# Results of six expert tiles kept in the join buffers, and another order of the row transfers on GpSimd, in a two-layer attention and mixture-of-experts kernel

## What is computed

```python
xn = _layernorm(x)
x = x + _L0_attn_ref(xn, ...) + _L0_ffn_ref(xn, ...)   # linear attention; top-2 of 8 experts, silu(hg) * hu, 176 wide, and a shared expert
xn = _layernorm(x)
x = x + _L1_attn_ref(xn, ...) + _L1_ffn_ref(xn, ...)   # masked linear attention per 256 tokens, rms norm, gate; top-2 of 8 experts, gelu, 512 wide
```

## Time and profile before

| | before |
|---|---|
| median of three runs | 919.67 us |
| profiled execution, its own time | 917.82 us |
| its span in the profile | 916.3 us |
| TensorE busy | 838.1 us, 91% |
| VectorE busy | 701.6 us, 77% |
| GpSimd busy | 625.9 us, 68% |
| ScalarE busy | 572.2 us, 62% |
| 224 sends, from L2014 | 220.8 us, 986 ns each |
| 136 returns, from L2116 | 151.8 us, 1117 ns each |
| 128 gathers, from L2025 | 132.7 us, 1036 ns each |

### The profile page before, as it was taken

One profiled execution on the slowest core, in us unless ns is written; L12 is line 12 of the kernel. 1 busy time (PEld: TensorE's weight loads), 2 busy tenths in 40 slices (PEclk: granted clock), 3 DMA queues, 4 the chain that ended last, 5 costly groups with the idle time before them and its releaser, 6 DMA issues.

```text
span 916.3 us, 22375 instructions
## 1 busy us (share of the span) xinstructions
PE 838.1 (91%) x7975; PEld 746.4 (81%) x7975; DVE 701.6 (77%) x1809; ACT 572.2 (62%) x1183; POOL 625.9 (68%) x607
## 2 busy tenths in 40 slices
PE   3789999999899999997998889888998899999997
PEld 3678878989799999985665566566898899999997
DVE  7687787886577998887898997897653556567786
ACT  5766465444466667769887776663664567566652
POOL 4157676777305888777888887886777777767663
PEclk9999999999999999999999999998999999999999
DMA  9799992115658998962111111116586778799996
GB/s 263 228 407 404 396 397 95 50 53 170 239 152 274 309 323 259 288 193 66 40 40 40 38 38 43 40 41 226 182 266 202 242 257 261 266 306 334 365 359 190
DMA packets 130990, 191.06 MB, mean 209 GB/s; under 512 B 15808, under 2 KB 85952, under 8 KB 130752
## 3 DMA queue, kind: packets, MB, share of 16 engines
q1 hardware_dynamic: 96720, 141.21, 46.1%
q0 software_dynamic: 16640, 34.37, 11.2%
q10 hardware_dynamic: 17520, 14.06, 4.8%
HBM read 110.74 MB, written 80.97 MB: 209 GB/s over the span
## 4 chain that ended last, share of the span: by engine, by line
PE 47%; DVE 23%; POOL 9%; issue 7%; DMA 6%; ACT 4%; SPq 4%; DVEq 0%; POOLq 0%; ACTq 0%
PE pair L888 11%; PE pair L835 4%; PE pair L834 4%; PE pair L836 4%; POOL sent L2014 3%; PE pair L755 3%; PE pair L865 3%; POOL ex_joined L2025 3%; DVE a_en L1578 2%; PE pair L668 2%; DVE X L1511 2%; PE pair L675 2%; DMA ex_stage<-in_experts 2%; DVE stats_t L1146 2%; PE pair L677 2%
## 5 line engine op out<-in xcount | busy, mean ns | idle before, releaser
L2014 POOL DMA_INDIRECT sent<-a_rows,slot x224 | 220.8, 986 | 81.1 <-issue 56.6
L2116 POOL DMA_INDIRECT back<-ex_tile_out,address x136 | 151.8, 1117 | 59.5 <-issue 32.6
L2025 POOL DMA_INDIRECT ex_joined<-outs,slot x128 | 132.7, 1036 | 81.7 <-DMA outs<-ex_tile_out 45.9
L834 PE MATMUL pair<-ex_x_hi,ex_w_hi 128*128 128x256 f32 x497 | 147.7, 297 | 0.0
L835 PE MATMUL pair<-ex_x_lo,ex_w_hi 128*128 128x256 f32 x497 | 141.7, 285 | 0.0
L836 PE MATMUL pair<-ex_x_hi,ex_w_lo 128*128 128x256 f32 x497 | 141.4, 285 | 0.0
L888 PE MATMUL pair<-ex_stage,ex_hid 128*128 128x128 f32 x1136 | 132.5, 275 | 0.0
L888 PEld LDWEIGHTS pair<-ex_stage,ex_hid 128*128 128x128 f32 x1136 | 129.9, 192 | 0.0
L1714 ACT ACTIVATE ex_w_hi<-ex_stage 128x768 fp32r<-128x768 f32 (+1 forms) x72 | 67.5, 937 | 91.0 <-DMA ex_stage<-in_experts 91.0
L1840 ACT ACTIVATE ex_hid<-pair,ex_stage 128x256 f32<-128x256 f32 x284 | 107.1, 498 | 0.1
L1349 DVE TENSOR_TENSOR ex_w_lo<-ex_stage,ex_w_hi 128x768 fp32r<-128x768 f32 (+1 forms) x72 | 77.4, 1075 | 36.2 <-ACT ex_w_hi L1714 35.6
(11 more groups left out here) (246 smaller groups left out, 1986.0 us busy)
## 6 DMA issues: line engine op xcount, KB each, us to landing
ex_stage<-in_experts SPq DMA_DIRECT2D x72, 578.0 KB, 5.6
outs<-v_heads SPq DMA_DIRECT2D x8, 4352.0 KB, 33.2
ex_stage<-in_experts SPq DMA_DIRECT2D x72, 320.0 KB, 4.9
ex_tile_in<-sent SPq DMA_DIRECT2D x72, 128.0 KB
outs<-ex_tile_out SPq DMA_DIRECT2D x71, 128.0 KB
ex_joined<-back ACTq DMA_DIRECT2D x15, 512.0 KB, 8.0
ex_tile_in<-sent SPq DMA_DIRECT2D x54, 132.0 KB
X<-in_x SPq DMA_DIRECT2D x16, 256.0 KB, 5.3
```

The source lines that it names most:

```text
L834: pe.matmul(o[:, of_half], wh, x_hi[i % 2][:, of_half], start=True, stop=False)
L2014: pool.indirect_dma_start(out=sent[layer], out_offset=bass.IndirectOffsetOnAxis(ap=slot_i[layer][k][:, s, j:j + 1], axis=0), in_=rows[laye ...
L2025: pool.indirect_dma_start(out=joined[g % NJOIN][:, j, k, :], out_offset=None, in_=outs, in_offset=bass.IndirectOffsetOnAxis(ap=slot_i[0][k ...
L2116: pool.indirect_dma_start(out=back, out_offset=bass.IndirectOffsetOnAxis(ap=address[i % NSIDE][:, s // HALF, s % HALF:s % HALF + 1], axis= ...
```

## The change

The results of tiles 0 to 5 of the second experts go to the six halves of the join buffers, those of later tiles to `tile_out` as before, so that `weigh1` waits for a return from tile 10 on (for that of tile n-4). The return addresses have 12 buffers in place of 6, the gates 2 in place of 6. The steps 4 to 16 of attention have 6 or 7 transfers in place of 8, the gathers begin one step earlier, and all 32 sends of the last super stand after attention, ahead of `give_back(0)`, without waits of their own.

```diff
-         {2: ((0, 0, 8),), 3: ((0, 8, 16),), 4: ((0, 16, 20),), 5: ((0, 20, 24),), 10: ((0, 24, 32),),
-          11: ((1, 0, 8),), 12: ((1, 8, 16),), 13: ((1, 16, 24),), 14: ((1, 24, 32),),
-          15: ((2, 0, 8),), 16: ((2, 8, 16),), 17: ((2, 16, 24),), 18: ((2, 24, 32),), 19: ((3, 0, 8),), 20: ((3, 8, 16),)})
-SENDS_LAST = {0: (3, 16, 24), 1: (3, 24, 27), 2: (3, 27, 30), 3: (3, 30, 32)}
+         {2: ((0, 0, 8),), 6: ((0, 8, 12),), 9: ((0, 12, 15),), 10: ((0, 15, 22),), 11: ((0, 22, 29),), 12: ((0, 29, 32), (1, 0, 4)),
+          13: ((1, 4, 11),), 14: ((1, 11, 18),), 15: ((1, 18, 25),), 16: ((1, 25, 32),),
+          17: ((2, 0, 8),), 18: ((2, 8, 16),), 19: ((2, 16, 24),), 20: ((2, 24, 32),)})
+SENDS_LAST = (3, 0, 32)
-NSTAGE, NIN, NOUT, NJOIN, NSIDE, AHEAD = (8, 4), 4, 4, 3, 6, 6
+NSTAGE, NIN, NOUT, NJOIN, NGATE, NADDRESS, AHEAD = (8, 4), 4, 4, 3, 2, 12, 6
+NEXTRA = 2 * NJOIN
-GATHERS = {4: ((11, 0, 4),), 5: ((11, 4, 8),), **{n - 6: ((n, 0, 8),) for n in range(12, 16)}}
+GATHERS = {3: ((11, 0, 8),), 4: ((12, 0, 7),), 5: ((12, 7, 8), (13, 0, 6)), 6: ((13, 6, 8),), 7: ((14, 0, 6),),
+           8: ((14, 6, 8), (15, 0, 4)), 9: ((15, 4, 8),)}
...
+        def home(i):
+            n = i - NTILES
+            return NOUT + n if 0 <= n < NEXTRA else i % NOUT
...
+        def results_of(i):
+            h = home(i) - NOUT
+            if h < 0:
+                return tile_out[home(i)][:]
+            return joined[h // 2][:].rearrange("p s k c -> p (s k) c")[:, SUB * (h % 2):SUB * (h % 2 + 1), :]
...
-                if n >= NSIDE:
-                    j = i - NSIDE
+                if n >= NADDRESS:
+                    j = i - NADDRESS
                     dve.wait_ge(results_dma(j), returned(j))
...
-                dve.wait_ge(results_dma(i - NOUT), returned(i - NOUT))
+                if n >= NEXTRA + NOUT:
+                    dve.wait_ge(results_dma(i - NOUT), returned(i - NOUT))
...
-            for n in range(NTILES):
-                if n in SENDS_LAST:
-                    s, first, end = SENDS_LAST[n]
-                    for i, jk in enumerate(range(first, end)):
-                        if n == 0:
-                            behind_tile1(i // NC1, i % NC1)
-                        else:
-                            behind_tile1(n + 1 + (i + 3) // NC1, (i + 3) % NC1)
-                        send(1, s, jk)
-                if n <= LAST_BACK:
-                    give_back(n)
+            s, first, end = SENDS_LAST
+            for jk in range(first, end):
+                send(1, s, jk)
+            for n in range(LAST_BACK + 1):
+                give_back(n)
```

More of the change, by code:

```diff
@@ L295, in build @@
         rms = sb("rms", [P, 2, 4, GT])
-        gate_t = [sb(f"gate_t{i}", [P, 4, 2, HALF]) for i in range(NSIDE)]
-        address = [sb(f"address{i}", [P, 2, HALF], I32) for i in range(NSIDE)]
+        gate_t = [sb(f"gate_t{i}", [P, 4, 2, HALF]) for i in range(NGATE)]
+        address = [sb(f"address{i}", [P, 2, HALF], I32) for i in range(NADDRESS)]
         sums_t = sb("sums_t", [P, 3 * P])
@@ L432, in build @@
         down_done, side_ready, out_ready = sem("down_done"), sem("side_ready"), sem("out_ready")
-        gathered_dma = [[sem(f"gathered_dma{i}{half}") for half in range(2)] for i in range(NJOIN)]
+        join_half_dma = [[sem(f"join_half_dma{i}{half}") for half in range(2)] for i in range(NJOIN)]
         joined_dma = [sem(f"joined_dma{i}") for i in range(NJOIN)]
@@ L472, in returns @@
             return halves(i) * (1 if i < NTILES else HALF)
+        def home(i):
[6 more added lines that the diff above has]
+            return joined[h // 2][:].rearrange("p s k c -> p (s k) c")[:, SUB * (h % 2):SUB * (h % 2 + 1), :]
         def results_dma(i):
-            return (put_dma, ret_dma)[i // NTILES][i % NOUT]
+            h = home(i) - NOUT
+            return (put_dma, ret_dma)[i // NTILES][home(i)] if h < 0 else join_half_dma[h // 2][h % 2]
         def returned(i):
-            return 16 * sum(returns(j) for j in range(i % NOUT, i + 1, NOUT) if j // NTILES == i // NTILES)
+            h = home(i) - NOUT
+            gathers = 0 if h < 0 else GT * len(range(h // 2, NG, NJOIN))
+            return 16 * (gathers + sum(returns(j) for j in range(i // NTILES * NTILES, i + 1) if home(j) == home(i)))
         def results_back(engine, i):
-            for j in range(i - NOUT + 1, i + 1):
+            for j in sorted({home(j): j for j in range(i // NTILES * NTILES, i + 1)}.values()):
                 engine.wait_ge(results_dma(j), returned(j))
@@ L901, in last_tokens @@
                         m = pe.matmul(bank[7][:, i * C:(i + 1) * C], is_of[:, SUB * (n - LAST_BACK - 1) + s, i * P:(i + 1) * P],
-                                      tile_out[(NTILES + n) % NOUT][:, s, :], start=(first and s == 0 and i == 0),
+                                      results_of(NTILES + n)[:, s, :], start=(first and s == 0 and i == 0),
                                       stop=(last and s == HALF * halves(n) - 1), skip_group_check=True)
@@ L1446, in side @@
                 r = tile_in[i // NTILES][i % NIN][:].rearrange("p (h s) c -> p h s c", h=2)
-                other, gate1, gate2, gate = (gate_t[i % NSIDE][:, k, :, :] for k in range(4))
+                other, gate1, gate2, gate = (gate_t[i % NGATE][:, k, :, :] for k in range(4))
                 mine = tile_first[:, 2 * n:2 * n + 2].unsqueeze(2).to_broadcast([P, 2, HALF])
                 dve.wait_ge(in_dma[i % NIN], 32 * (i // NIN + 1))
-                if n >= NSIDE:
-                    j = i - NSIDE
+                if n >= NADDRESS:
+                    j = i - NADDRESS
                     dve.wait_ge(results_dma(j), returned(j))
@@ L1456, in side @@
                 dve.tensor_tensor(gate, gate1, gate2, ALU.add)
-                dve.scalar_tensor_tensor(address[i % NSIDE][:], other, 0.0, r[:, :, :, TOK2], ALU.not_equal, ALU.add).then_inc(side_ready, 1)
+                dve.scalar_tensor_tensor(address[i % NADDRESS][:], other, 0.0, r[:, :, :, TOK2], ALU.not_equal, ALU.add).then_inc(side_ready, 1)
             def hidden0(n, c):
@@ L1505, in collect0 @@
             def collect0(g, half):
-                dve.wait_ge(gathered_dma[g % NJOIN][half], 16 * GT * (g // NJOIN + 1))
+                dve.wait_ge(join_half_dma[g % NJOIN][half], 16 * GT * (g // NJOIN + 1))
                 for k in range(K):
@@ L1847, in results0 @@
                 a = slice(0, SLOTS * halves(i))
-                act.activation(flat(tile_out[i % NOUT][:])[:, a], bank[7][:, a], ACT.Copy).then_inc(out_ready, 1)
+                act.activation(flat(results_of(i))[:, a], bank[7][:, a], ACT.Copy).then_inc(out_ready, 1)
             for n in range(NTILES + 1):
@@ L2115, in give_back @@
                         behind_tile1(n + 2, s - 1)
-                    pool.indirect_dma_start(out=back, out_offset=bass.IndirectOffsetOnAxis(ap=address[i % NSIDE][:, s // HALF, s % HALF:s % HALF + 1], axis=0),
-                                            in_=tile_out[i % NOUT][:, s, :], in_offset=None).then_inc(ret_dma[i % NOUT], 16)
+                    pool.indirect_dma_start(out=back, out_offset=bass.IndirectOffsetOnAxis(ap=address[i % NADDRESS][:, s // HALF, s % HALF:s % HALF + 1], axis=0),
+                                            in_=results_of(i)[:, s, :], in_offset=None).then_inc(results_dma(i), 16)
             for m in range(EX_GATHERS * GT * K):
```

10 lines of the change are left out of this document (5 added, 5 removed).

## The result

The changed kernel takes **927.45 us** (median of 20 runs, 921.22 to 936.99). The kernel before took 920.18 beside it (20 runs). The ratio is 1.0062, with an interval of 1.0045 to 1.0079: 4 to 7 us slower, 5.7 by the ratio. The medians alone lie 7.3 apart; the ratio leaves out one slow run of the changed kernel. The direction was forecast, the size was not: 17.4 us forecast, about 6 measured. The time lies inside the range of 925 to 944 us, near its lower end.

The account below looks back on a forecast made before the run. Took VectorE as the full engine in attention behind 486 us and TensorE as the bound in the second experts after the first ten tiles; +18.4 at the experts' start and -1 in attention made +17.4, 937.1 us, range 925 to 944.

Parts of the forecast that it names:

- What is on the path of that is what TensorE waited for: Attention steps 4 to 16: sixteen fewer transfers save only TensorE's mask wait, -1 us, bounds -5.1 and +8.
- GpSimd has full hands there and nobody waits for them: Second attention, behind 486 us: GpSimd is busy but not binding; TensorE waited for masks only 1.7 us in all.
- What is late next is VectorE, which loses no instruction: Attention steps 4 to 16: with fewer transfers VectorE is late next, its instructions unchanged; part of the -1 us term.
- Rival A: Attention gives it back: GpSimd's work sets the step, each of 16 transfers saves 1.27 us; 917.8 us; chance 7%.
- Rival C: Attention: earlier GpSimd masks meet VectorE's additions more often in steps 6 to 10, +8 us, 945 us; chance 10%.
- Rival B: Start of second experts: only all_sent binds, returns of tile 6 land in time; +4.9, 924.6 us; chance 7%.
- The order behind attention: Behind the last power: 48 sends ahead of give_back(0) in place of 24, so it begins at 715.5 us, 33 later.
- all_sent: Second experts: the last send begins 5.9 us later, so tile 10's transposes come at 722.9 us, 13.6 late.
- The extra buffers: Second experts: first return wait at weigh1(10), 759.2 us; tile 14 26.1 us late, restart 1.5, less 9.2: +18.4 us.
- The lower bound of +8.3: Start of second experts: at 1.27 us a transfer throughout, tile 14's transposes 17.5 us late, giving +8.3.
- the sentence on the Trainium skill ("DMA: Bandwidth & Descriptors", anatomy of one DMA on the software path): Landing of a return: 2.2 us estimated for 64 KB, making the sum +15.1; the trace's 5.5 was taken instead.
- The sign expected in attention: Attention: steps 4 to 16 as long as before but for step 7; steps near 13 us would point to Rival A.

Follow-up runs that it names:

- fifth experiment: Changed kernel with the transfer tables of before and 16 sends ahead of all returns, plus collect0 of groups 11 to 15 making 4 of 8 additions: 914.24 us, ratio 0.9911.
- seventh experiment: Changed kernel with seven transfers in steps 4 and 6 to 10, ten in 17 and 18, eight elsewhere, 18 sends ahead of returns: 914.85 us, ratio 0.9937.
- fourth experiment: Changed kernel with eight transfers again in steps 13 to 16 and 28 sends ahead of the returns: 921.42 us, ratio 1.0022.
- first experiment: Changed kernel with the transfer tables of before (eight transfers in every step) and 16 sends ahead of all returns: 913.63 us, ratio 0.992.

## Why the prediction was right in direction and wrong in size

**The step that failed** is the first one: "What is on the path of that is what TensorE waited for", with -1 us taken and -5.1 as the far bound. It was -6.7 us in the first eight steps, outside both. The premise "GpSimd has full hands there and nobody waits for them" took waits of others as the only sign of a bound. But GpSimd ran 14.3 us of work a step without a wait, and a step can't be shorter than what an engine does in it. I had the rows: 17.2 of 20 us busy is full once the 0.3 us between two transfers are added. The slack of 2.0 us ahead of TensorE hid it. VectorE was then nearly as slow, since the instructions of L1511 and L1156 took long, and so hardly anyone ran up against the masks. With VectorE relieved (fifth experiment), the slack went and the pace of the roots stayed. "What is late next is VectorE, which loses no instruction" was right in the instructions and wrong in their length: they got shorter (470 to 395 ns over all 64, 499 to 237) as GpSimd had less to do. The Trainium skill ("SBUF — State Buffer", two separate sides) has a VectorE instruction with two SBUF inputs and a GpSimd instruction that reads SBUF lock a shared port pair; the lengths agree, but no run here took the meetings away by themselves.

**Rival A** had the mechanism and a chance of 7%. Its price, 1.27 us for each of 16 transfers, was too high, since a step gets shorter only down to the pace of the other engines. In steps 6 to 10 five transfers fewer made 71.4 us into 67.4, 0.8 each, and the three more that the changed kernel takes out there gave nothing. Step 4 gained 1.5 us for its one transfer. Step 5 gained 1.2 (13.30 us from root to root before, 12.13 in the changed kernel, 13.34 with eight transfers in the seventh experiment), although it has no power of the deviation: what counts is the room that the others leave. Step 11 gained nothing (13.3 and 13.4 from root to root), and nor did steps 13 to 16, 52.4 us before and 52.1 after: the fourth experiment put four transfers back and lost nothing there. **Rival C** went the other way, with shorter instructions. **Rival B** did not come: weigh1(10) waited.

**The order behind attention** was right: the first return 65.7 us behind the first send forecast, 66.1 measured. **all_sent** was right: tile 10's transposes 8.75 us behind the start of the last send forecast, 8.4 measured; 13.6 us late forecast, 15.0 measured.

**The extra buffers**: the place was right, and the stage's start was 4 us dearer in the forecast than it was. weigh1(10) came 38.2 - 35.9 = 2.3 us earlier for the returns, to which I gave 1.415 us each and which took 1.33. It came 3.2 earlier for the landing: 5.5 us taken, 2.26 measured (746.01 to 748.27 us). Of these 5.5 us 1.3 were lost again, since tile 4's transposes stood 17.1 us behind the first send in place of 18.3 and a tile took 6.85, so that full pace itself was earlier; another 0.4 went with the later first return. The stage's start, +27.6 less 9.2 in the prediction, was 23.7 less 9.6. The lower bound of +8.3 had left out the restart of 1.5 that the forecast contains; with it the bound is +9.8. Here the sentence on the Trainium skill ("DMA: Bandwidth & Descriptors", anatomy of one DMA on the software path) had the better figure, 2.2 us, against rows that I had taken from another situation (below).

Most signs expected in the experts were seen: the 48 sends in a row, the stall of tile 10 (14.9 us idle, some 13 forecast), that of tile 14 (5.5 idle, about 10 forecast), no wait at weigh1(4) to (9). The sign expected in attention, steps as long as before but for step 7, failed, and one named as a sign against the forecast came: steps near 13 us. The forecast's attention term was off by 5.7 us and the start by 4.3, both toward too slow a kernel. The rest, some 2 us, is within what the medians can tell and has no cause shown. That the time fell inside the range is not to the forecast's credit: the range was wide enough for rivals, and the step of attention on which the forecast rested was wrong.

## What to carry to other kernels

An engine that never waits can set the pace even if hardly anybody is seen to wait for it: add up what it does in one step, gaps of the queue included, and set that against the step. Work moved off such an engine pays only down to the next engine's pace (here 0.8 us for each of the first five transfers in steps 6 to 10, nothing for the four in steps 13 to 16), while at its new place each can cost its full length (start +14.1 us with 48 sends ahead and -6.5 with 32: 1.29 each). Where two limits lie behind each other, lifting one gives nothing: the buffers alone gave 0, and with the sends ahead of the returns 7 us, in the kernel with the old tables. No variant with all additions was clearly faster than that one.

## What the hardware showed that I had not expected

**A return landed later where the DMA engines carried more.** The kernel before, in the stretch of the return that landed after 5.5 us (windows; PEclk, DMA share and GB/s are last):

```profile
686.00:692.00 6.00, 6.00 (x55) 6.00 (x54) 0.59 (x6) 4.08 (x10) 4.48 (x6) 1.00 0.70 255
```

The changed kernel where it landed after 2.26 us:

```profile
745.00:749.00 4.00, 1.43 (x13) 1.24 (x12) 0.70 (x2) 0.00 (x0) 3.09 (x4) 1.00 0.20 66
```

In the first, a tile's weights and rows were under way. In the second, weights for the next tile stood behind the very weigh1 that waited. In the first experiment it was 2.26 us too for tile 10. For tile 11, whose weights had just been asked for, its last return at 736.45 us was followed by weigh1 at 741.55. All eight kernels whose first wait for a return lasted 6.4 us or more agree: that return landed after 2.25 to 2.64 us at a DMA share of 0.15 to 0.20, and the last return of the tile behind it after 4.97 to 5.45 at 0.90 to 0.96. No run changed the load by itself. The stall matters by its length: in the kernel before, the last loads had been issued from 685.09 us on, just ahead of the return of 686.58; in the changed kernel from 735.84 on, 10 us ahead of that of 746.01. A stall that lasts long enough lets the loads run out, and then the landing to be taken is that of a quiet DMA.

**Some executions lose up to 1.6 and 2.7 us where the clock is lower.** In the kernel before, 560 to 570 and 630 to 640 us:

```profile
560.00:570.00 10.00, 8.28 (x96) 5.20 (x89) 6.81 (x22) 3.73 (x7) 6.49 (x7) 0.83 0.10 32
630.00:640.00 10.00, 6.57 (x104) 5.44 (x108) 5.88 (x18) 0.87 (x2) 5.91 (x7) 0.75 1.01 371
```

In the first experiment, which has the same attention:

```profile
560.00:570.00 10.00, 8.27 (x115) 5.43 (x107) 7.66 (x22) 5.15 (x10) 8.07 (x9) 1.00 0.13 41
630.00:640.00 10.00, 5.73 (x136) 4.59 (x128) 7.77 (x22) 2.21 (x4) 6.37 (x8) 1.00 0.92 305
```

Part of the time TensorE ran at 1.2 GHz in place of 2.4 there; in the second window, ahead of its matmul of 631.02 us, it had stood idle for 1.64 us behind VectorE. In the first experiment it stood idle as long at the same place (ahead of its matmul of 632.98 us), and the clock stayed at 1.00. Step 12 took 15.6 us with the first and 14.0 without, the last two 25.4 and 22.6. It need not cost anything: in the fifth experiment the clock was 0.83 from 560 to 570 us as well, and the roots of step 12 stood 13.76 us apart, 13.78 in the first. Of the 11.5 us by which attention seemed to get shorter, 4.5 are of these three steps. What makes the clock fall in one execution and not in the other stays open.
